# The opening of a two-layer graph kernel: who issues the zero fill, when the roots run, and in which order the first group is worked

## The reference

```python
deg = jax.ops.segment_sum(w_all, dst_all, num_segments=N)      # edge weights, and 1 for the node's own loop
deg_inv_sqrt = jnp.where(deg > 0, jax.lax.rsqrt(deg), 0.0)
norm = deg_inv_sqrt[src_all] * w_all * deg_inv_sqrt[dst_all]
xp = x @ W
msg = xp[src_all] * norm[:, None]
out = jax.ops.segment_sum(msg, dst_all, num_segments=N)
...
x = _layernorm(x + relu(out + b), axis=-1)
```

## Time and profile before

| | |
|---|---|
| median of 3 runs | 1240.66 us (1238.07 to 1240.92) |
| profiled execution | 1237.18 us |
| its span | 1235.4 us |
| busy: PE, PEld, DVE, ACT, POOL | 81%, 64%, 68%, 57%, 53% |
| mean granted TensorE clock | 0.908 of full |
| moved | 289 MB, 234 GB/s over the span |

### The profile page before, as it was taken

How to read it: one execution, slowest core, us unless ns; L and a number is a source line. 1 busy time by engine, 2 the same in 40 slices (tenths; PEclk the granted TensorE clock), 3 DMA queues, 4 the chain that set the end, 5 groups by cost and what they waited for, 6 DMA issues and landing times.

```text
span 1235.4 us, 23211 instructions
## 1 busy us (share of the span) xinstructions
PE 1004.6 (81%) x5088; PEld 788.5 (64%) x5088; DVE 840.1 (68%) x2538; ACT 699.5 (57%) x1632; POOL 657.0 (53%) x812
## 2 busy tenths in 40 slices
PE   6579998988749999999994788888888888834443
PEld 6557776776538888888883566666666666523332
DVE  7588777767327777777774566666566666448887
ACT  0168778867626666666663344343444434358887
POOL 2048888888547777777775455555555554310000
PEclk9999999989859999999998899999999999955555
DMA  9949999999976888888886678787777877579998
GB/s 359 419 147 242 242 253 231 248 236 237 214 177 212 271 283 277 282 279 279 278 276 213 178 176 182 170 171 178 168 173 176 183 168 155 77 204 348 349 350 296
DMA packets 175015, 289.00 MB, mean 234 GB/s; under 512 B 18514, under 2 KB 75750, under 8 KB 174966
## 3 DMA queue, kind: packets, MB, share of 16 engines
q1 hardware_dynamic: 120982, 176.23, 41.9%
q0 software_dynamic: 35840, 83.91, 36.0%
q10 hardware_dynamic: 18144, 28.32, 6.1%
HBM read 139.49 MB, written 148.90 MB: 233 GB/s over the span
## 4 chain that ended last, share of the span: by engine, by line
PE 28%; issue 18%; POOL 11%; DMA 5%; DVE 4%; ACT 4%; POOLq 2%; SPq 2%; DVEq 0%; ACTq 0%
PE bank L1079 6%; PE bank L1090 4%; PE bank L1100 4%; POOL tiny L463 3%; DMA node_mem<-sum 3%; PE bank L1088 3%; PE bank L1102 3%; PE bank L1103 3%; POOL tiny L466 3%; PE bank L1072 2%; PE bank L1086 1%; PE bank L1080 1%; POOL G_lo L476 1%; POOL tiny L470 1%; POOL tiny L468 1%
## 5 line engine op out<-in xcount | busy, mean ns | idle before, releaser
L500 POOL DMA_INDIRECT sum<-R_mem,l_sidx x80 | 127.9, 1599 | 173.7 <-ACT R_mem L636 167.4
L449 POOL DMA_INDIRECT sum<-R_mem,sidx_all x80 | 131.1, 1639 | 51.1 <-issue 29.3
L1052 PE MATMUL bank<-W0h,G_hi 128*128 128x512 f32 x320 | 134.0, 419 | 0.9 <-ACT G_lo L600 0.9
L1052 PE MATMUL bank<-W0h,G_lo 128*128 128x512 f32 x320 | 126.6, 396 | 0.0
L1052 PE MATMUL bank<-W0l,G_hi 128*128 128x512 f32 x320 | 126.3, 395 | 0.0
L611 ACT ACTIVATE node_mem<-node_mem,tiny 128x512 f32<-128x512 f32 x80 | 65.4, 817 | 91.2 <-POOL tiny L472 91.2
L476 POOL TENSOR_TENSOR G_lo<-node_mem,G_hi 128x512 fp32r<-128x512 f32 x80 | 104.1, 1301 | 19.4 <-ACT G_hi L607 19.4
L875 DVE SCALAR_TENSOR_TENSOR edge_mem<-edge_mem,Y,bank 128x128 f32<-128x128 f32 x240 | 73.1, 388 | 57.2 <-ACT edge_mem L630 42.5
L630 ACT COPY edge_mem<-bank 128x256 f32<-128x256 f32 x80 | 29.8, 372 | 135.8 <-PE bank L1090 135.8
L979 PE MATMUL bank<-G_hi,M_mem 128*128 128x512 f32 x200 | 88.4, 442 | 17.3 <-ACT R_mem L544 15.7
L492 POOL DMA_INDIRECT G_mem<-x_d,dst_i x80 | 79.5, 993 | 35.4 <-issue 16.2
(11 more groups left out here) (172 smaller groups left out, 2995.7 us busy)
## 6 DMA issues: line engine op xcount, KB each, us to landing
sum<-zeros ACTq DMA_DIRECT2D x42, 512.0 KB
filt_d<-node_mem SPq DMA_DIRECT2D x40, 512.0 KB
node_mem<-sum SPq DMA_DIRECT2D x80, 256.0 KB, 2.7
G_mem<-x SPq DMA_DIRECT2D x80, 256.0 KB, 2.8
x_d<-node_mem SPq DMA_DIRECT2D x80, 256.0 KB, 2.1
node_mem<-filt_d SPq DMA_DIRECT2D x80, 256.0 KB
sum<-node_mem SPq DMA_DIRECT2D x80, 192.0 KB, 2.3
out<-G_mem SPq DMA_DIRECT2D x20, 512.0 KB, 4.2
```

The costliest lines, as they stand in the source:

```text
L449: pool.indirect_dma_start(sum0, bass.IndirectOffsetOnAxis(ap=sidx[:, t:t + 1], axis=0), R[t % 8][:, :], None, compute_op=ALU.add).then_inc ...
L500: pool.indirect_dma_start(sum1, bass.IndirectOffsetOnAxis(ap=l1_sidx[:, t:t + 1], axis=0), R3[t % 8][:, :], None, compute_op=ALU.add).then ...
L1052: ins = pe.matmul(bank[4 + a][:, :], zt[b][:, c * P:(c + 1) * P], w[:, c, :], start=(c == 0 and k == 0), stop=(c == 3 and k == 2))
```

## The change

It touches only the opening and the first group. ScalarE issues 8 of the 42 zero fills (NZ = 8) and SyncE the other 34, behind all its loads and the first two `fT` blocks. ScalarE's roots wait for the steps of `s_const` that they need (4 and 6 instead of 11). VectorE's chain to `dis` becomes `inverse_root`, which runs after the src counts of s = 0; `rn`, `Y` and the scaled copies of W1s and W2s move behind the group loop. TensorE waits for `s_dis` at the first look-up and no longer before its first index rows. In step 2 TensorE's first two sums of group 0 stand ahead of the index rows, and ScalarE's copies of them ahead of its copy of those rows. In step 1 VectorE does `M` and `G_lo` before the dst counts and the src counts. The bytes moved and what is computed are the same.

```diff
+        NZ = 8
+
+        def zero_rows(j):
+            return sum0[j * 256:(j + 1) * 256, :].rearrange("(p r) d -> p (r d)", r=2)
...
             for c in range(4):
                 sp_.dma_start(W0_s[c], W0[c * P:(c + 1) * P, :]).then_inc(s_wres, 16)
-
-
-            for s in range(T4 + 3):
+            for s in range(2):
+                sp_.dma_start(fT[s][:, :], rbf[:, s * Q:(s + 1) * Q]).then_inc(w_fT[s], 16)
+            sp_.wait_ge(s_zero, 1)
+            for j in range(NZ, 42):
+                sp_.dma_start(zero_rows(j), zeros[:, :]).then_inc(s_zero0, 16)
+
+
+            for s in range(2, T4 + 3):
...
-                    if s >= 2:
-                        sp_.wait_ge(w_pre, s - 1)
+                    sp_.wait_ge(w_pre, s - 1)
...
-            with act.Fori(0, 42) as j:
-                act.dma_start(sum0[bass.ds(j * 256, 256), :].rearrange("(p r) d -> p (r d)", r=2), zeros[:, :]) \
-                   .then_inc(s_zero0, 16)
+            for j in range(NZ):
+                act.dma_start(zero_rows(j), zeros[:, :]).then_inc(s_zero0, 16)
             act.wait_ge(s_wres, 64)
             for c in range(4):
                 act.copy(W0h[:, c, :], W0_s[c]).then_inc(s_whi, 1)
-            act.wait_ge(s_const, 11)
+            act.wait_ge(s_const, 4)
             act.activation(degs[:, :], degm[:, :], ACT.Sqrt).then_inc(s_sqrt, 1)
+            act.wait_ge(s_const, 6)
             act.activation(rn[:, :], rsq[:, :, 0], ACT.Sqrt).then_inc(s_sqrt, 1)
...
+                if s == 2:
+                    sums_out(0, 3, 0)
+                    sums_out(1, 2, 1)
                 if s < T4:
                     act.wait_ge(e_row, s + 1)
...
                 if s >= 2:
                     if g >= 2:
                         act.wait_ge(e_scat, 64 * (g - 1))
-                    sums_out(0, 3, 0)
-                    sums_out(1, 2, 1)
+                    if g:
+                        sums_out(0, 3, 0)
+                        sums_out(1, 2, 1)
...
             dve.wait_ge(s_deg_mm, T + 1)
             link(dve.tensor_scalar(deg[:, :], bank[6][:, 0:T], 1.0, None, ALU.add))
             link(dve.tensor_scalar(degm[:, :], deg[:, :], 1e-34, None, ALU.max))
-            link(dve.tensor_scalar(deg[:, :], deg[:, :], 0.0, None, ALU.is_gt))
             link(dve.tensor_tensor(rsq[:, :, 0], rsq[:, :, 0], rsq[:, :, 1], ALU.add))
             link(dve.tensor_tensor(rsq[:, :, 0], rsq[:, :, 0], rsq[:, :, 2], ALU.add))
-            for q in range(2):
-                k = Y0 / (16.0 * C ** 0.5) if q == 0 else 1.0 / (16.0 * C ** 0.5 * 3.0 ** 0.5)
-                dve.wait_ge(s_loadw, 16 * 11)
-                link(dve.tensor_scalar(W1s_s[:, q, :], W1s_r[:, q, :], k, None, ALU.mult))
-            link(dve.tensor_scalar(W2s_s[:, :], W2s_r[:, :], 1.0 / C ** 0.5, None, ALU.mult))
+            link(dve.tensor_scalar(deg[:, :], deg[:, :], 0.0, None, ALU.is_gt))
             link(dve.tensor_copy(degt[:, :], degm[:, :]))
-            dve.wait_ge(s_sqrt, 2)
-
-            link(dve.reciprocal(dis[:, :], degs[:, :]))
-            link(dve.reciprocal(rn[:, :], rn[:, :]))
-            link(dve.tensor_tensor(degt[:, :], degt[:, :], dis[:, :], ALU.mult))
-            link(dve.tensor_tensor(degt[:, :], degt[:, :], dis[:, :], ALU.mult))
-            link(dve.tensor_scalar(degt[:, :], degt[:, :], -0.5, 1.5, ALU.mult, ALU.add))
-            link(dve.tensor_tensor(dis[:, :], dis[:, :], degt[:, :], ALU.mult))
-            link(dve.tensor_tensor(dis[:, :], dis[:, :], deg[:, :], ALU.mult))
-            link(dve.scalar_tensor_tensor(Y[:, :, :], rij[:, :, :], Y1, rn[:, :].unsqueeze(2).broadcast_to([P, T, 3]),
-                                          ALU.mult, ALU.mult))
-            dve.sem_inc(s_dis, 1)
...
+            def inverse_root():
+                dve.wait_ge(s_sqrt, 1)
+
+                link(dve.reciprocal(dis[:, :], degs[:, :]))
+                link(dve.tensor_tensor(degt[:, :], degt[:, :], dis[:, :], ALU.mult))
+                link(dve.tensor_tensor(degt[:, :], degt[:, :], dis[:, :], ALU.mult))
+                link(dve.tensor_scalar(degt[:, :], degt[:, :], -0.5, 1.5, ALU.mult, ALU.add))
+                link(dve.tensor_tensor(dis[:, :], dis[:, :], degt[:, :], ALU.mult))
+                link(dve.tensor_tensor(dis[:, :], dis[:, :], deg[:, :], ALU.mult))
+                dve.sem_inc(s_dis, 1)
...
+                def counts0():
+                    dve.wait_ge(e_trow, g + 1)
...
+                def counts1():
+                    dve.wait_ge(s_srow, s + 1)
+                    if s >= 1:
+                        dve.wait_ge(w_dup, 4 * s)
...
-                if s >= 1:
...
-                if s < T4:
...
+                if s == 0:
+                    counts1()
+                    inverse_root()
+                if s >= 2:
+                    counts0()
+                    if s < T4:
+                        counts1()
                 if s >= 1:
                     if g >= 2:
                         dve.wait_ge(e_mm, 4 * (g - 1))
+                    dve.wait_ge(e_trow, g + 1)
                     for q in (3, 2, 1, 0):
...
                         dve.scalar_tensor_tensor(G_lo[t % 8][:, :], G0[t % NG], coef[:, t:t + 1], G_hi[t % 8][:, :].bitcast(F32),
                                                  ALU.mult, ALU.subtract).then_inc(e_lo, 1)
+                    if s == 1:
+                        counts0()
+                        counts1()
                     dve.wait_ge(e_dup, 4 * (g + 1))
...
+            dve.wait_ge(s_sqrt, 2)
+            link(dve.reciprocal(rn[:, :], rn[:, :]))
+            link(dve.scalar_tensor_tensor(Y[:, :, :], rij[:, :, :], Y1, rn[:, :].unsqueeze(2).broadcast_to([P, T, 3]),
+                                          ALU.mult, ALU.mult))
+            dve.wait_ge(s_loadw, 16 * 11)
+            for q in range(2):
+                k = Y0 / (16.0 * C ** 0.5) if q == 0 else 1.0 / (16.0 * C ** 0.5 * 3.0 ** 0.5)
+                link(dve.tensor_scalar(W1s_s[:, q, :], W1s_r[:, q, :], k, None, ALU.mult))
+            link(dve.tensor_scalar(W2s_s[:, :], W2s_r[:, :], 1.0 / C ** 0.5, None, ALU.mult))
...
-            pe.wait_ge(s_dis, 1)
-
             pe.wait_ge(s_wTc, 3)
...
+                if s == 2:
+                    sums(0, 3, 0)
+                    sums(1, 2, 1)
                 if s < T4:
                     if s:
...
-                if s >= 2:
+                if s >= 3:
                     sums(0, 3, 0)
                     sums(1, 2, 1)
+                if s >= 2:
                     pe.wait_ge(w_h, g + 1)
                     filter_mm(0)
...
                     if s:
                         pe.wait_ge(s_pick, 4 * s)
+                    else:
+                        pe.wait_ge(s_dis, 1)
                     for v in range(4):
...
-            pe.wait_ge(s_const, 11)
+            pe.wait_ge(s_const, 19)
```

22 lines of the change are left out of this document (9 added, 13 removed).

## The result

The changed kernel takes 1225.82 us (median of 4 runs, 1224.40 to 1226.57); the kernel before took 1240.26 us in the runs beside them (1238.07 to 1240.92). The ratio is 0.9885, 95% interval 0.9868 to 0.9902: 14.4 us less, by the medians. The forecast was 1229.7, in a range of 1223.0 to 1234.5. The two gains differ because the profiled execution of before (1237.18 us) was 3.1 us faster than the median of its runs, while the changed kernel's was 0.6 us faster. In the profile the sum is near, but two of its terms are not, and they have opposite signs.

A forecast was written before the change was run, and what follows sets the result against it. GpSimd's scatter chain was taken to bound the first edge stage, group 0's fourth scatter setting the end. Terms -14.1 + 4.1 - 1.0 = -11.0 us gave 1229.7 us; own range 1228.2 to 1230.7, wide range 1223 to 1234.5 (about 0.85).

The forecast's parts named there:

- The fourth scatter of group 0 decides the end: First edge stage: time saved ahead of GpSimd's fourth scatter is saved once at the end; savings behind it are not.
- The rest is shift: From the fourth scatter to the end, everything was to stay unchanged except for moving earlier.
- Roots freed, -14.1: Opening: ScalarE's roots no longer behind the fills, second root at 48.15 instead of 62.36; first look-up pick 14.1 us earlier.
- The stall in the degree loop, +4.1: VectorE's one-hot instructions lose 4.1 us beside GpSimd's four W0l subtractions, one instruction passing per GpSimd instruction.
- Rival 1: No stall in the degree loop: gain 15.1, 1225.6 us; up to 18.3 if idle time goes too; chance 0.3.
- t0 = 62.4: t0 is the pick of the look-up giving the first coefficients; forecast at 62.4 us, stall included, against 72.37 before.
- if the degree loop ends as before: Condition on the look-up pick at 58.3 us: last one-hot tile still at 45.7, before adding the 4.1 us stall.
- The order, -1.0: New order in group 0: counted from the look-up pick, first scatter 4.8 us sooner, fourth only 1.0 us sooner.
- The fill costs nothing: Zero fills moved to SyncE: the landing was to hold the fourth scatter to 78.3 at most, under its 82.6; cost zero.
- Landed by about 71: Zero fill and the gathers competing with it, worked by bytes at full DMA rate, were to land by about 71 us.
- Rival 2: Fourth result of group 0 later through TensorE blocks or a ScalarE copy: gain 6 to 9, 1231.7 to 1234.7; chance 0.12.
- Rivals 3 and 4: Fill lands late: 0.03 slower (1244.4 and up), 0.04 no change; roots not freed: gain 1.0, 1239.7 us, chance 0.01.

The follow-up runs named there:

- e5: The changed kernel again with no edit; 1224.43 us, ratio 0.9886 to the kernel before.
- e9: e7 with ScalarE, not SyncE behind the fill, loading the third group's radial rows (fT) after its Relu of step 0; 1221.01 us, ratio 0.9855.
- e10: e9 without the split: the first scatter waits for all 42 zero fills as in the changed kernel; 1224.81 us, ratio 0.9884.
- e1: The kernel before with only the change's new order of group 0; 1238.01 us against 1239.63, ratio 0.9990.
- e11: The kernel before again with no edit, for one profile; 1238.64 us in one run.
- e6: The changed kernel with e4's split fill wait, and GpSimd's W0l subtraction held until VectorE has done the degree vectors; 1229.41 us, ratio 0.9920.
- e7: e6 with VectorE's inverse root moved ahead of step 0; 1228.46 us, ratio 0.9924.
- e2: The changed kernel with the new order of group 0 undone; 1231.09 us, ratio 0.9927.
- e4: The changed kernel with fills reordered and their wait split: first scatter waits for 23, group 4 for the other 19; 1230.07 us, ratio 0.9928.
- e8: The changed kernel with all 42 zero fills on SyncE behind its weight loads, none on ScalarE (NZ = 0); 1228.58 us, ratio 0.9913.

## Why the prediction was right or wrong, step by step

**The fourth scatter of group 0 decides the end: right.** Thirteen profiles hold it within 2.9 us. "The rest is shift" is slightly too simple: the spans behind an early fourth scatter are longer (1143.0 to 1143.8 in after, e5, e9, e10) than behind a late one (1141.6 to 1142.2 in before, e1, e11), so 1 to 2 us of such a gain are given back; e6 and e7, at 1143.9 and 1141.0 on one chip, show the scatter of this number.

**Roots freed, -14.1: right.** The second root ran at 48.34 (48.15 forecast).

**The stall in the degree loop, +4.1: right in cause and size.** Without the subtraction the last one-hot instruction starts at 41.83 to 42.36 (e6, e7, e9, e10), with it at 46.04 and 46.06: 3.7 to 4.2 us. The four stretched instructions show the form forecast, one of VectorE for one of GpSimd. The Trainium skill's rule on the shared port pair ("SBUF — State Buffer", "Who interferes with whom") had spoken for it with one tensor input too, and the trace agrees: 1.26 to 1.33 us. Rival 1, no stall, is refuted, although its price, 1225.6, is the nearest to the measured time.

**t0 = 62.4: wrong, it was 59.24.** The step that failed is "if the degree loop ends as before", to which the 4.1 were added: the loop of before had 3.3 us of idle time in its middle that this profile did not have, so it ended at the same place with the stall in it. The last one-hot instruction started at 46.04, where 45.86 + 4.1 = 50.0 was forecast. The prediction had this time only in rival 1, as something that a shorter backlog might cure. The runs show that it comes and goes in one and the same kernel; why TensorE and VectorE stop there stays open. TensorE's own gaps are partly put down to "issue" (1.2 us in e2), VectorE's to "remote" (2.3 us in e2 and e4), and no row explains either. One rival was not looked at: the page lists two DMA queues of kind "instruction" (0.28 and 0.26 MB), and whether what they bring came late while the DMA engines were full (share 1.02 to 1.04 in these windows) was not tried. A smaller error went the other way. The look-up was taken at 1.16 us from its start to the pick; it took 2.03 (57.21 to 59.24), 0.9 us more, since its eight products took 2.00 us and not 1.12. That short time is special to the profile that the prediction read; e9 alone comes near it. With the idle time t0 was 64.7 (e4), 2.3 us later than forecast: these 0.9, and 1.5 in the loop.

**The order, -1.0: too small, it is 2.0 to 2.6.** One part is a misread row. The prediction let the fourth scatter start 0.86 us behind the *end* of the fourth copy. Where a scatter really waits for a single copy, it starts 0.86 behind its *start* (73.19 to 74.05 in e9). That is 0.59 us of it; the rest was not taken apart. By this, the results of the changed kernel allowed its fourth scatter at 78.16 + 0.86 = 79.02, that is t0 + 19.8 against 20.2 forecast.

**The fill costs nothing: wrong.** "Landed by about 71" is where nearly all its bytes were through. But the scatter waits for the last of them, and the working by bytes at full rate had no term for a thin rest such as the windows above show up to 73.0. The first scatter's wait ended at 73.76, or, less the 0.86 of an issue, at 72.9 (an estimate). With t0 at 62.4 it would have been hidden. At 59.24 it held the first scatter 3.9 us: sidx was written from 68.89 on, and in e4, where nothing else was waited for, the scatter started 0.99 behind that (74.32 to 75.31), so 69.9 against 73.76. The fourth it held 0.7 us, from 79.02 to 79.69. The prediction's own rule for this case, that a late landing sets the first scatter and the first the fourth, was the right one in form (5.93 us between them here, 6.42 forecast); on a landing 1.9 us too early it found that the fill costs nothing for t0 at 58.3 as well.

**Sum.** Forecast: -14.1 + 4.1 - 1.0 = -11.0. Measured at the fourth scatter: t0 -13.13 (had the loop had its idle time here too, the gain would have been at least 3.3 us less), from t0 on -0.73 (order and fill together), -13.86; at the end of the span -12.0. That the profile came out near is luck: two errors of opposite sign, 3.1 us at t0 and 1.9 given back behind it. By the timer they cancel less: 1225.82 us, and all four runs, lie below the forecast's own 1228.2 to 1230.7, though inside the wide range.

**Rival 2** (fourth result late) did not come in this kernel: +18.9 to the copy's start. It did in e6 and e7, by a load and not by TensorE's order. **Rivals 3 and 4** did not come in it either; e8 shows a small rival 3.

## What to carry to other kernels

When a stage is paced by one engine's queue, follow the *last* item of its first group and check it against every run: the first item can move by 8 us and the end go the other way. When a start is pulled forward, list every load that sits behind bulk traffic in the same queue, with the time at which it lands; those times don't move forward with the work, they can even move back when the work's own traffic now runs beside the bulk (the radial rows in e6 and e7), and each becomes a bound in turn, here the fill and then 40 KB of radial rows. And idle time, or a short duration, in a profile is part of a baseline only if a second profile of the same kernel has it.

## What the runs showed of the hardware that was not expected

- Between 13 and 18 us VectorE stood still for 2.9 to 3.9 us and TensorE for 2.4 to 3.4 in five of thirteen profiles, in the middle of the degree loop, in kernels whose instructions on these two engines don't differ up to there. In each of the three groups, each on one chip, either all profiles had it or none. The timer fits a cost where the loop is on the path: e4, with it in its profile, took 1230.07, and the changed kernel on another chip, without it, 1224.43. It does not prove it, since e4 also has the split wait.
- In the changed kernel the eight look-up matmuls took 2.00 us in step 1, though TensorE was busy in all of 60 to 65 us, and 1.12 us 11 us later, with the granted clock at 1.00 in both stretches:

```profile
63.78 2.00 PE L1052 MATMUL bank<-dis,edge_mem 128*128 128x80 f32 x8
...
75.10 1.12 PE L1052 MATMUL bank<-dis,edge_mem 128*128 128x80 f32 x8
```

  Those of step 0 took 1.99 or 2.00 us in ten of the thirteen profiles, 1.67 in e6, 1.18 in e9 and 1.12 in the first profile of before. So idle time ahead of them is not enough to make them slow. In e6 and e7 the product that followed the wait for the load took 2.04 us, and there the granted clock does show 0.50 (1.2 GHz); why the same lengths stand beside a clock of 1.00 elsewhere is open.

- An instruction of VectorE with one tensor in and one out in SBUF (128x80 or 128x128, f32) takes 1.15 to 1.33 us instead of 0.2 to 0.3 beside a TENSOR_TENSOR of GpSimd. Beside GpSimd's issuing of gathers it keeps its 0.3.
